# Cross-attention and expert feed-forward kernel: three zero fills moved in the start-up, four filler matmuls and two GpSimd waits removed

## The reference

```
# layer 1: gated linear attention over the context, per batch
gates  = concat(q, k, v) @ [ig|fg] + bias           # 4 heads
F      = cumsum(log_sigmoid(fgate));  g = igate - F
D      = exp(F_s - F_t + ig_t - rowmax)             # causal 512 x 512 per head
C      = (q k^T / 8) * D;  h = C / max(|sum C|, exp(-max)) @ v
x      = x + groupnorm(h) * outnorm_weight
# layer 2
n1     = layernorm(layernorm(x)) * g1 + b1
probs  = softmax(mean(n1) @ rw + rb)                # 2 mixtures
for m in 0, 1:  q, k, v = n1 @ wq, wk, wv + biases  # 16 heads of 16
                out_m = softmax(q k^T / 4) v @ wo + bo
x      = x + sum_m probs_m * out_m
n2     = layernorm(x) * g2 + b2
top 2 of 8 experts by softmax(mean(n2) @ ffn_rw):   x + sum p_e * gelu(n2 @ w1_e) @ w2_e
```

## Time and profile before

| | us |
|---|---|
| median of 3 runs | 1379.91 |
| range of the runs | 1379.36 to 1380.89 |
| the profiled execution's own time | 1379.36 |
| its span, first to last instruction | 1377.6 |
| PE busy in the span | 1327.6 (96%) |
| DVE busy | 1082.6 (79%) |
| ACT busy | 892.6 (65%) |
| POOL busy | 368.9 (27%) |

### The profile page before, as it was taken

One profiled execution on the slowest core, in us unless ns is written; L12 is line 12 of the kernel. 1 busy time (PEld: TensorE's weight loads), 2 busy tenths in 40 slices (PEclk: granted clock), 3 DMA queues, 4 the chain that ended last, 5 costly groups with the idle time before them and its releaser, 6 DMA issues.

```text
span 1377.6 us, 23095 instructions
## 1 busy us (share of the span) xinstructions
PE 1327.6 (96%) x7549; PEld 654.9 (48%) x7674; DVE 1082.6 (79%) x2371; ACT 892.6 (65%) x1696; POOL 368.9 (27%) x371
## 2 busy tenths in 40 slices
PE   9998899999999999999999999999999999999999
PEld 6643434454444544445434554445444454343356
DVE  6889988978779787987789787797869887786721
ACT  4257667775687657685677756776577755757761
POOL 8511333215213141223312152130512223122000
PEclk9999999999999999999999999999999999999999
DMA  4012112211221213211132112222031211212002
GB/s 121 17 51 81 42 52 95 79 47 39 99 79 65 69 37 118 71 62 55 48 111 82 44 43 93 76 73 70 28 127 47 85 55 43 80 34 92 17 1 92
DMA packets 96657, 90.23 MB, mean 65 GB/s; under 512 B 20833, under 2 KB 91617, under 8 KB 95645
## 3 DMA queue, kind: packets, MB, share of 16 engines
q1 hardware_dynamic: 96540, 88.75, 19.5%
HBM read 35.05 MB, written 4.25 MB: 29 GB/s over the span
## 4 chain that ended last, share of the span: by engine, by line
PE 38%; DVE 6%; issue 2%; ACT 2%; SPq 2%; POOL 0%; DMA 0%; DVEq 0%; another core or an unknown queue 0%; ACTq 0%; POOLq 0%
PE psum L904 6%; PE psum L919 6%; PE psum L873 5%; PE psum L854 5%; PE psum L889 4%; DVE mx L1428 4%; PE psum L736 3%; PE psum L498 3%; SPq L2043 2%; ACT prob L1748 1%; PE psum L771 1%; PE psum L521 1%; PE psum L609 1%; PE psum L582 0%; DVE resid L1299 0%
## 5 line engine op out<-in xcount | busy, mean ns | idle before, releaser
L1748 ACT ACTIVATE prob<-psum 128x512 f32<-128x512 f32 x1024 | 553.7, 604 | 295.6 <-PE psum L919 209.1
L1428 DVE TENSOR_REDUCE mx<-psum 128x1 f32<-128x512 f32 x1024 | 640.0, 680 | 55.0 <-PE psum L889 52.9
L904 PE MATMUL psum<-qst,kst 128*128 128x512 bf16 x901 | 270.6, 382 | 18.1 <-issue 9.5
L919 PE MATMUL psum<-prob,vst 128*17 128x512 f32 x2048 | 246.4, 595 | 1.4 <-ACT prob L1748 1.1
L889 PE MATMUL psum<-kst,qst 64*128 64x512 bf16 x1024 | 176.6, 383 | 16.2 <-DVE resid L1299 5.2
L889 PEld LDWEIGHTS psum<-kst,qst 64*128 64x128 bf16 x1024 | 48.5, 93 | 206.3 <-issue 171.3
L904 PEld LDWEIGHTS psum<-qst,kst 128*128 128x128 bf16 x1024 | 82.1, 98 | 131.1 <-issue 76.8
L1898 POOL CAST parts<-resid 128x512 bf16<-128x512 f32 x64 | 39.7, 620 | 248.3 <-DVE resid L1299 248.3
L873 PE MATMUL psum<-w,cxT 128*128 128x256 f32 x448 | 105.8, 382 | 0.0
L919 PEld LDWEIGHTS psum<-prob,vst 128*17 128x17 f32 x2048 | 45.8, 96 | 122.3 <-issue 97.9
L854 PE MATMUL psum<-n2T,x 128*128 128x512 f32 x224 | 102.5, 597 | 0.0
(11 more groups left out here) (250 smaller groups left out, 1698.9 us busy)
## 6 DMA issues: line engine op xcount, KB each, us to landing
kst<-parts SPq DMA_DIRECT2D x372, 64.0 KB, 2.0
qst<-parts SPq DMA_DIRECT2D x372, 64.0 KB, 2.0
cmat<-G_dram SPq DMA_DIRECT2D x7, 1024.0 KB, 4.7
x<-in_L_ffn_fw SPq DMA_DIRECT2D x14, 512.0 KB, 3.3
w<-in_L_ffn_fw SPq DMA_DIRECT2D x14, 512.0 KB, 4.3
xbuf<-in_x SPq DMA_DIRECT2D x8, 512.0 KB, 4.6
kin<-in_ctx SPq DMA_DIRECT2D x8, 512.0 KB, 3.7
out<-acc SPq DMA_DIRECT2D x7, 512.0 KB, 3.0
```

Of the source, the lines that this page charges most:

```text
L904: e.matmul(psum[:, u.bank, :], kst[:, par, h // 2, g * P:(g + 1) * P], qst[:, par, h // 2, :], start=True, stop=True).then_inc(u.full, 1)
L919: ins = e.matmul(psum[32 * j:32 * j + VW, VB, :], vst[:, g, h, :], prob[:, g % 2, j, :], start=g == 0, stop=g == NT - 1, tile_position=(0, ...
L1428: e.tensor_reduce(mx[:, qq, par, j, t:t + 1], psum[:, u.bank, :], AX, ALU.max).then_inc(u.free, 1)
L1748: e.activation(prob[:, g % 2, j, :], psum[:, u.bank, :], ACT.Exp).then_inc(u.free, 1)
```

## The change

- The fill of `kst` (L1047) goes from behind M to the end of `gate_columns`, ahead of L1025.
- The fill of the first half of `qst` (L1189) goes from behind s1 to behind "lf", between L1029 and L1033.
- The fill of the second half of `qst` (L1213) goes from behind s2 to behind M, the place that the `kst` fill had.
- The semaphore `cleared` goes; both `qst` fills count on `ones`, for which SP now waits at 5 ahead of the first write of ones.
- The two `keep_clock(2)` around `max_rows(0, 0)` go.
- `make_choice` no longer waits for L1025 between its halves.
- The last batch's residual sum on POOL no longer waits for n2.

```diff
-        cleared = sem("cleared")
@@ PE, ahead of period 0
-            keep_clock(2)
             max_rows(0, 0)
-            keep_clock(2)
@@ DVE, stage_a, batch 0
                 e.scalar_tensor_tensor(out=lf, in0=gf, scalar=0.0, in1=ga, op0=ALU.min, op1=ALU.subtract
                                        ).then_inc(va.here("lf", b), 1)
+                if b == 0:
+                    e.memset(qst[HALVES[0], 1, HP:], 0.0).then_inc(ones, 1)
                 yield "F"
@@
                 e.tensor_tensor(rows[:, 2, :], gf, rows[:, 1, :], ALU.add).then_inc(va.here("M", b), 1)
                 if b == 0:
-                    e.memset(kst[HALVES[0], 1, HP:], 0.0).then_inc(ones, 1)
+                    e.memset(qst[HALVES[1], 0, HP:], 0.0).then_inc(ones, 1)
@@
                     residue(b, n)
                 if b == 0:
-                    e.memset(qst[HALVES[0], 1, HP:], 0.0).then_inc(cleared, 1)
                     u = uses["pick", 1, 0, 0]
@@
                     residue(b, 2)
-                    e.memset(qst[HALVES[1], 0, HP:], 0.0).then_inc(cleared, 1)
@@ DVE, gate_columns
                     ins.then_inc(gate_setup, 1)
+                e.memset(kst[HALVES[0], 1, HP:], 0.0).then_inc(ones, 1)
@@ POOL, make_choice
                 for which in range(2):
-                    if which:
-                        e.wait_ge(*va.at("a1", 0))
@@ POOL, ending
                 yield "summed"
-                e.wait_ge(*vc.at("n2", b))
@@ SP
-                    e.wait_ge(cleared, 2)
                     stack(b, 3)
@@
-            e.wait_ge(ones, 3)
+            e.wait_ge(ones, 5)
```

## The result

The changed kernel took 1389.08 us (median of 4 runs, 1388.16 to 1391.44), the kernel before 1379.63 us on the same chip (4 runs): the ratio is 1.0078, with a 95% interval of 1.0058 to 1.0097. It is slower, by 9.45 us median less median. The ratio is not the quotient of these two medians: it draws on all 13 executions of the changed kernel on record and stands for 10.8 us (8.0 to 13.4). The ratios further down, too, differ a little from the quotients of their medians. The forecast was slower too, but by 3.0 us: the direction was right, the size a third of what came, and 1389.08 lies outside the range of 1380.3 to 1385.2.

What follows compares the result with a forecast made beforehand. The prediction took PE (96% busy) to pace the periods and DVE's list to be critical in the start-up from L1029 to the columns. Terms of +2.37 us plus 0.90 for the clock, on 1379.36, gave 1382.6 us; range 1380.3 to 1385.2.

Steps and rivals of the forecast that it cites:

- The fill that leaves s1: Start-up, PE's first maximum: without DVE's fill, ACT's copy ends last, so only 0.04 us is gained, not 3.12.
- The fill that leaves s2: Period 0: DVE starts on the first maxima earlier, so PE's projection L736 loses its wait, -1.06 us.
- The four fillers at the router: Round `max_rows`: without the first pair the transposition starts 0.09 us sooner; the second pair is worth nothing.
- the clock falls at the router too: Rival: PE, sparse without the router's fillers, loses clock there; +1.5 us on the forecast, 1384.1 us, chance 0.20.
- `make_choice` without its wait: Start-up: POOL's copies run beside L1025 and gain nothing; L1025 could lengthen by 0.10 us, taken as 0.
- The sum on POOL: Ending: the sum runs beside DVE's four n2 operations; at most 0.92 us against 1.51 of slack, taken as 0.
- the sum on POOL blocks n2: Rival, ending: n2 ends at 1337.82, PE's means start 0.9 us later; 1383.5 us, chance 0.10.
- PE's clock at the first place: Start-up, after the 20 fillers: PE idles 3.4 us and its clock falls; +0.90 us, between 0 and 1.9.
- absorbed: Rival: another wait behind the start-up takes up one to two us, or the clock stays up; 1380.2 us, chance 0.16.
- faster: Rival: the fills leaving s1 and s2 pay in full, sum -3.0 us; 1376.4 us, chance 0.06.
- Theory A: Posed for the experiments: the two dropped waits are free, as forecast, and the clock alone makes the difference.
- Theory B: Posed for the experiments: the waits kept POOL away from DVE; their loss costs some 2 us each beside the clock.

Runs made afterwards that it cites:

- b_fills27: The kernel before with only the three fills moved (and the count of `ones`) and 27 instead of 20 filler matmuls ahead of the spread of G: 1382.27 us, 1.0020.
- a_choice: The changed kernel with only the wait of POOL's copies for L1025 put back: 1387.76 us, 1.0056 against the kernel before.
- a_router: The changed kernel with only the two pairs of filler matmuls round `max_rows` put back: 1390.31 us, 1.0071 against the kernel before.
- a_n2: The changed kernel with only the wait for n2 ahead of POOL's sum in the ending put back: 1388.22 us, 1.0060 against the kernel before.
- a_fill31: The changed kernel with 31 instead of 20 filler matmuls ahead of the spread of G: 1386.94 us, 1.0052 against the kernel before.
- b_norouter: The kernel before with only the two pairs of filler matmuls round `max_rows` taken out: 1379.32 us, 0.9999.
- b_nochoice: The kernel before with only POOL's wait for L1025 between the two halves of its copies taken out: 1382.05 us, 1.0020.
- b_non2: The kernel before with only the ending's wait for n2 ahead of POOL's sum taken out: 1381.71 us, 1.0014.
- b_fills: The kernel before with only the three fills moved, 20 filler matmuls as before: 1385.77 us, 1.0028.
- b_idle5: The kernel before with 8 instead of 20 filler matmuls ahead of the spread of G and nothing else: 1384.57 us, 1.0023.

## Why the forecast was right in direction and wrong in size

By the steps of the prediction:

- **What a fill costs, 3.13 us: right.** b_fills27 as a whole came to the sum within its interval (+2.28 for +2.46).
- **The fill of `kst`, +0.43 for L1025: right.** 14.99 was forecast and is 14.99.
- **The fill of `qst` behind "lf", +3.13: right.** Between F and the L1026 ahead of it stand 4.02 us now and 0.82 before, 3.2 more.
- **The fill that leaves s1, -0.04: right.** The first PE maximum is as late as all that stands ahead of it (+10.18 against +10.21), and nothing of the 3.12 us came back; in b_fills27 it is +3.62 against +3.66. DVE now waits there for PE, as it had no reason to before:

```profile
74.10 0.69 DVE L1190 CAST qst<-psum 128x512 bf16<-128x512 f32 x1 [2.58 <-PE psum L680]
```

- **The fill that leaves s2, -1.06: right for the fill, and lost again in the changed kernel.** From the router's matmul to the projection are 6.66 us before. They are 5.58 in a_choice and in a_router, a gain of 1.08. In the changed kernel they are 6.58.
- **The four fillers at the router: wrong by the clock.** That is where the 1.0 us of the line above went. The rival "the clock falls at the router too" came true in this profile; the forecast had given it 0.20. The window of the changed kernel behind the router, and PE's transposition, which has an idle time ahead of it and still comes no sooner behind the maxima than before (0.33 us behind the start of `mxx`, as in the earlier trace rows):

```profile
90.70:94.00 3.30, 3.30 (x16) 1.50 (x14) 1.12 (x4) 1.76 (x4) 1.76 (x2) 0.54 0.24 81
...
88.08 0.27 PE L497 MATMUL psum<-ident,mxx 128*32 128x128 f32 x1 [0.75 <-DVE mxx L1430]
```

  It is not a certain loss: a_choice, a_n2 and a_fill31 have no such fillers either and kept their clock there. b_norouter lost it for 3.3 us, and router to projection are 6.66 us as before, as DVE's fill behind s2 still stood at that place and covered it. The -0.09 is not there at all. a_router, with the fillers put back, shows no gain in time (1.0071 against 1.0078), so what they are worth in the median is not shown.
- **`ones` at 5 and `cleared`: nothing, right.** In the list of waits of SP's queue of the changed kernel (us in total, times, longest) the load of the next context waits for the second statistics, and no line of the list names a fill:

```profile
SPq L2023 <- DVE stats_a L1161: 42.9, 1, 42.9
```

- **`make_choice` without its wait: wrong, +2.1 us instead of 0.** This is a failed step: the prediction asked only who waits for POOL. DVE's own delay it bounded by a neighbouring row, 0.10 us, then took as 0, and it named no rival for it. That row, L1029 at 0.78 us from 17.97, met only the last 0.27 us of the copies; it was no measurement of this pair. The operation beside the copies took 2.54 us in b_nochoice (L1025) and 2.77 in the changed kernel (L1022), for 0.68. b_nochoice gives +1.87 us at the next DVE operation and +2.06 in the median; a_choice takes 2.15 off at L1026.
- **The sum on POOL: wrong, +0.65 us at PE's mean, +1.7 in the median of b_non2, instead of 0.** The bound of 0.92 us from L1340 was no bound. L1340 is the same operation of DVE, but in six of its seven groups of four POOL did nothing beside it; only the seventh had a partner, two `tensor_scalar` of 128x256 (L1961), and took 1.86 us for 1.37. So the row hardly measured a pair at all. The slack of 1.51 us was right: 2.02 us of blocking less 1.51 are 0.51, and PE's mean came 0.65 later. The rule of the Trainium skill that the prediction quoted (SBUF — State Buffer, "Who interferes with whom") gave n2's end as start + 1.38 + 2.35; the trace has 3.40 in place of 3.73, so it agrees within 0.33 us. The same section says that a DVE instruction with two SBUF inputs contends with a GpSimd instruction that reads SBUF, and that is L1022's case (2.77 us for 0.68); the prediction held the section against one of the two dropped waits only. The rival "the sum on POOL blocks n2" came true; it named 0.9 us, and the direct part is 0.65.
- **PE's clock at the first place, +0.9 us (0 to 1.9): wrong, and the largest part.** This is the other failed step: the mechanism was named and its size was some 4.4 us. Two reasons. The low clock was taken to last a stretch of 3.4 us or at most the four L695; it lasts 10.2 us in b_fills and 13.7 in the changed kernel, into the 32 matmuls of L581, for which L1083 waits. And the prediction priced PE's work only as far as the columns, though PE's next products are on the path as soon as PE is later than DVE. Of the 10.21 us at the second L1083, L1026 accounts for 2.52 and the fill for 3.20; of the remaining 4.5 us the fillers of a_fill31 take off 4.3. Besides, 2.1 us of blocking lengthened PE's idle time from 3.1 to 5.16 us. That this made the low clock last longer is not shown: with 5.14 us idle it lasted 10.2 us in a_router, as long as with 3.11 in b_fills.
- **PE's clock at the end: not foreseen.** Behind the late n2 the grant fell once more in this profile, 1349.8 to 1353.2, and the last batch's transpositions took 1.81 us where they had 1.07:

```profile
1350.20:1353.50 3.30, 3.30 (x14) 3.09 (x14) 0.75 (x4) 2.76 (x3) 0.00 (x0) 0.54 0.00 0
```

  a_choice has the same blocked n2 (3.41 us) without that fall, and its block of expert products (L853) follows n2 1.36 us sooner.
- **The rivals "absorbed" and "faster": neither came.** The delay is 10.10 us at the projection behind the router (95.97 for 85.87) and 10.23 at n2, so the eight periods absorbed nothing.

Put together from the parts timed alone, in medians: the fills with 20 fillers +4.45, the choice +2.06, n2 +1.72, the router 0 (-0.67, within its interval): 8.2 of the 9.45 us. What is left is within the uncertainty of such a sum, and its cause stays open. The changed kernel's profile, 12.3 us above that of before, adds up by steps: `kst` fill +0.4, L1022 held +2.1, fill behind "lf" +3.2, clock up to the second L1083 +4.5, fill of s2 gone -1.1, clock at the router +1.0, the periods +0.1, n2 held +0.65, clock behind n2 +1.45.

Theory A falls with b_nochoice and b_non2. Theory B holds for the choice, which costs some 2 us without any clock. For n2 the blocking itself costs 0.65 us, and the rest of what the profile shows is the clock behind it. In this profile the clock has 6.9 us and the blocking 2.7; the medians are not fine enough to split them so.

## What to carry over

A gap of DVE is free only ahead of the instruction that waits in it: a fill of one size cost 0.33 us on one side of an operation and 3.2 on the other. A semaphore wait that nobody's data needs may still keep two engines from getting in each other's way; before it goes, lay the two engines' timelines over each other, and bound the price by the partner's whole duration (of the series, if it is one), not by a similar row with another partner. Where a delay opens an idle stretch on PE, price the low clock over all of PE's work until it has come back (here 10 to 14 us), and move the fillers along with the delay.

## What the runs showed of the hardware

- 24 casts of 128x64 on POOL, back to back, held a DVE operation with two inputs from 14.57 on: 2.54 instead of 0.68 us. Eight copies went by before it came in. In the changed kernel the same operation took 2.77, and the series was over by then (11.46 + 5.79 = 17.25).
- Four `tensor_scalar` of 128x256 f32 took 3.40 us beside one `tensor_tensor` of 2.35 us on POOL, 1.38 alone, in five kernels alike (3.40 or 3.41: the changed one, a_choice, a_fill31, a_router, b_non2).
- PE idle for 4.9 us in b_idle5 and busy behind it: the grant fell at 20.4, inside the gap, and stayed at 0.50 for 10.2 us (to 30.6); the first two L695 took 2.07 us for 1.02. Filler matmuls over the same stretch kept it at 1.00. The low stretch also had 10.2 us in b_fills, a_choice, a_n2 and a_router (PE idle for 3.04 to 5.14 us), and 13.7 in the changed kernel. A gap of 1.43 us at the same place, in b_nochoice, cost no clock.
- The length of a low stretch and its place differ between executions of one kernel: in the executions behind the ratios the kernel before was granted 0.993 to 0.999 on the mean, the changed one 0.989 to 0.994.
